# First attention: the value products of four key blocks placed one at a time between the score steps

## What is computed

```python
Q, K, V = (proj(W_Q), proj(W_K), proj(W_V))          # 16 heads of 16 features
Q = _apply_rope(Q, cos, sin); K = _apply_rope(K, cos, sin)
scores = jnp.einsum('bhsd,bhtd->bhst', Q, K) / jnp.sqrt(jnp.float32(D_K))
scores = jnp.where(causal[None, None], scores, -jnp.inf)
attn = jax.nn.softmax(scores, axis=-1)
out = jnp.einsum('bhst,bhtd->bhsd', attn, V)
```

## Time and profile before

| | us |
|---|---|
| median of 3 runs | 1461.62 |
| lowest, highest | 1457.1, 1462.15 |
| profiled execution | 1458.09 |
| its span | 1456.4 |

### The profile page before, as it was taken

How to read it: one execution, slowest core, us unless ns; L and a number is a source line. 1 busy time by engine, 2 the same in 40 slices (tenths; PEclk the granted TensorE clock), 3 DMA queues, 4 the chain that set the end, 5 groups by cost and what they waited for, 6 DMA issues and landing times. The chain is left out here.

```text
span 1456.4 us, 29479 instructions
## 1 busy us (share of the span) xinstructions
PE 1237.8 (85%) x9695; PEld 969.9 (67%) x9696; DVE 850.5 (58%) x1794; ACT 660.5 (45%) x1260; POOL 666.6 (46%) x616
## 2 busy tenths in 40 slices
PE   5886999999978959944998786798869999999996
PEld 3664555555547747732766666788847888878885
DVE  4897788888738849985554684433323333333332
ACT  2881666666755534420445552233213433333332
POOL 6865777776351304876000000454224554444553
PEclk9996899999999968775999998999979999999998
DMA  2487999999300025654442420000174334554331
GB/s 54 141 277 248 259 285 270 274 275 286 69 1 1 1 82 162 195 159 91 111 110 51 144 73 8 18 26 30 37 285 133 57 60 127 134 133 131 56 50 20
DMA packets 122865, 179.26 MB, mean 123 GB/s; under 512 B 26052, under 2 KB 83820, under 8 KB 122772
## 3 DMA queue, kind: packets, MB, share of 16 engines
q1 hardware_dynamic: 105876, 159.62, 37.6%
q0 software_dynamic: 16896, 18.44, 7.5%
HBM read 104.73 MB, written 74.31 MB: 123 GB/s over the span
## 5 line engine op out<-in xcount | busy, mean ns | idle before, releaser
L1635 DVE TENSOR_REDUCE att_top<-att_psS 128x4 f32<-128x512 f32 (+2 forms) x192 | 195.0, 1037 | 45.2 <-PE att_psS L1522 42.2
L2786 POOL DMA_INDIRECT out<-ffn1c_y,ffn1c_table x72 | 113.4, 1575 | 180.4 <-ACT ffn1c_y L2899 112.3
L2927 DVE TENSOR_TENSOR ffn1c_hid<-ffn1c_psG,ffn1c_sil 128x512 f32<-128x512 f32 x72 | 49.8, 692 | 145.6 <-PE ffn1c_psG L2827 145.6
L1606 ACT ACTIVATE att_prob<-att_psS 128x1024 f32<-128x1024 f32 (+1 forms) x96 | 83.3, 887 | 63.0 <-PE att_psS L1536 63.0
L1516 PE MATMUL att_psS<-pairs_ka,pairs_qa 48*128 48x384 f32 (+3 forms) x512 | 100.0, 399 | 11.8 <-DMA pairs_ka<-k_parts 7.2
L2827 PE MATMUL ffn1c_psG<-ffn1c_w_h,ffn1c_xh 128*128 x288 | 98.0, 422 | 11.1 <-DMA ffn1c_w_l<-experts_lo 6.0
L2435 POOL DMA_INDIRECT slots<-ffn1b_entry,ffn1b_sloti x64 | 62.9, 983 | 92.1 <-ACT ffn1b_act_h L2648 52.6
L1606 ACT ACTIVATE pairs_part<-att_psS 128x1024 f32<-128x1024 f32 (+1 forms) x96 | 83.0, 889 | 35.8 <-PE att_psS L1536 35.8
L2775 POOL DMA_INDIRECT ffn1c_rows<-normed_rows,ffn1c_table x72 | 71.2, 988 | 46.6 <-DVE ffn1c_gate L2947 22.9
L2827 PE MATMUL ffn1c_psG<-ffn1c_w_l,ffn1c_xh 128*128 x288 | 91.4, 399 | 0.0
L2827 PE MATMUL ffn1c_psG<-ffn1c_w_h,ffn1c_xl 128*128 x288 | 91.1, 398 | 0.0
(11 more groups left out here) (397 smaller groups left out, 3518.4 us busy)
## 6 DMA issues: line engine op xcount, KB each, us to landing
prep_raw<-in_w_all SPq DMA_DIRECT2D x27, 512.0 KB, 5.6
experts_hi<-ffn0w_room SPq DMA_DIRECT2D x27, 512.0 KB, 5.9
experts_lo<-prep_lo SPq DMA_DIRECT2D x27, 512.0 KB, 7.4
ffn1c_w_h<-experts_hi SPq DMA_DIRECT2D x8, 1536.0 KB
ffn1c_w_l<-experts_lo SPq DMA_DIRECT2D x8, 1536.0 KB
qkv_near<-near_keys SPq DMA_DIRECT2D x32, 320.0 KB, 4.3
q_parts<-pairs_part SPq DMA_DIRECT2D x8, 1024.0 KB
k_parts<-pairs_part SPq DMA_DIRECT2D x16, 512.0 KB
```

Of the source, the lines that this page charges most:

```text
L1606: act.activation(dst, src, ACT.Exp, scale=0.25).then_inc(s["exp"], 1)
L1635: dve.tensor_reduce(dst, src, AX.X, ALU.max).then_inc(s["max"], 1)
L2786: pool.indirect_dma_start(out=rows_out, in_=y[:, t.buf, :], in_offset=None, out_offset=bass.IndirectOffsetOnAxis(ap=table[:, t.value:t.val ...
L2927: dve.tensor_tensor(hid[:, t.par, :], psG[:, t.par, 1, :], sil[:, t.par, :], ALU.mult).then_inc(s["act"], 1)
```

## The change

In TensorE's loop, the value products of blocks 1 and 2 get places of their own. Before, blocks 0 and 1 stand together behind query step 5, and blocks 2 and 3 together behind query step 2 of the next round. After, block 0 stands behind query step 5, and blocks 1, 2 and 3 behind query steps 0, 1 and 2 of the next round; each is followed by the key step of the same n. Nothing else changes.

```diff
                     if n == 5 and 0 <= u - 3 < NU:
                         values(u - 3, 0)
-                        values(u - 3, 1)
-                    if n == 2 and 0 <= u - 4 < NU:
-                        values(u - 4, 2)
-                        values(u - 4, 3)
+                    if n < TG - 1 and 0 <= u - 4 < NU:
+                        values(u - 4, n + 1)
                     if 0 <= u - 3 < NU:
                         key_scores(u - 3, n)
```

## The result

The changed kernel takes 1466.84 us in the median of 11 runs (1459.38 to 1477.65), the kernel before 1461.62 in as many (1456.9 to 1464.01). The ratio is **1.0046**, 95% interval 1.0028 to 1.0063: 5.2 us slower by the medians and 6.7 by the ratio, with 4.1 to 9.2 us as its interval: outside the noise of so many runs, and too near to half a per cent to say on which side it lies. The forecast was 1466. The profiled execution took 1467.21 us, its span is 1465.5.

What follows compares the result with a forecast made beforehand. TensorE's own occupancy was taken as the bound. +0.38 us a unit gave +10.3 over 27 periods; with -2.5, -2.0 and +0.4 that is +6.2 us, put at 1466 us between two starting points, range 1456 to 1476.

Steps and rivals of the forecast that it cites:

- The bound: Attention stage: TensorE's own occupancy, about 8.05 us of each 8.49 us unit, sets the pace; two places wait.
- the period: Sign of being right: copies at L1612 some 8.8 to 8.9 us apart, where they are 8.49.
- 0.175 us in a group: Fixed cost of each group of value products, whatever it holds; four groups instead of two add 0.35 us a unit.
- 0.12 at the entry: Extra time from marks into a value group rather than a score step; two more entries add 0.24 us a unit.
- Exits: Rival: leaving a value group also costs 0.10, two more a unit, 1471 to 1473 us; chance 0.10.
- The two waits: TensorE's waits at query step 1 and key step 3 shrink, giving back 0.10 and 0.11 us a unit.
- The offsets: Savings over the stage against the longer units: irregular units -2.5 us, the drain at its end -2.0 us.
- the half-clock start: First value products run at half clock, where two more groups cost again: +0.4 us.
- Free groups: Rival: added groups cost nothing, a unit is at best 8.28 us, total 1456 to 1457 us; chance 0.22.
- The late clock: Rival: block 0 alone fails to bring full clock, up to 7.6 us per unit, about 1474 or 1489; chance 0.12.
- POOL: Block 2, wanted 1.14 us sooner, might wait for POOL's clip: taken as 0, between 0 and 0.3 us.

Runs made afterwards that it cites:

- half_marks: Changed kernel with one of the two halves of the causal marks left out, 16 matmuls fewer a unit: 1445.87 us, kernel before 1442.4.
- rows_late_before: Kernel before, with VectorE's two instructions on the turned maxima moved from behind its step 1 to behind step 2: 1468.93 us, kernel before 1465.59.
- one_group: Kernel before, with all four value blocks in one group behind query step 2 of the next round: 1514.29 us, kernel before 1465.59.
- both halves: Kernel before with only block 1 moved behind query step 0, or only block 2 behind query step 1: 1468.5 and 1467.92 us, kernel before 1465.59.
- turn_between: rows_late_before with the turning of the maxima put between value blocks 2 and 3: 1440.44 us, kernel before 1442.4.
- block1_moved: Kernel before with only block 1 moved, behind query step 0, blocks 2 and 3 still together: 1468.5 us, kernel before 1465.59.
- rows_late_after: Changed kernel with VectorE's two instructions on the turned maxima behind its step 2: 1462.06 us, kernel before 1437.44.

## Why the prediction was right

- **The bound.** TensorE's occupancy plus one wait for VectorE: shown by half_marks and rows_late_before. one_group adds what the sum did not need: this holds only while no group is longer than the ring can cover. Of the signs set down beforehand, the period did not come: 8.715 us, where 8.8 to 8.9 was to show it right.
- **0.175 us in a group:** the four groups of a unit take 2.82 against 2.50, +0.32 for a forecast of +0.35. **0.12 at the entry:** 0.22 and 0.22 at the new places, +0.22 against 0.24. **Exits:** nothing, key step 2 after a group still 0.28; that rival falls.
- **The two waits** are the terms that were mis-sized. Query step 1 gave back 0.17 and not 0.10: I had taken the whole of its 0.65 us as its own, but its first part had waited too (0.23 where 0.13 is enough). Key step 3 gave back 0.17 and not 0.11; the maximum of step 2 begins 0.34 behind its marks (378.49 to 378.83), and I had 0.40, read at step 0. So a unit is +0.225 and not +0.38, and 27 of them 6.1 us and not 10.3.
- **The offsets** were over-counted as well, which is why the total held: irregular units gave back 0.7 and not 2.5, the drain 0.9 and not 2.0. In the drain ScalarE's period hardly moved (6.34 against 6.38): one block less stands before step 5, but the same block then stands before step 0. Only the end, 5.04 against 5.97, kept its 0.9. The total of the stage, 4.5, and the median's 5.2 against a forecast of 6.2 and a centre of 4.4 above the median, is a sum in which two errors of 4.2 and 2.9 us stood against each other (and 0.4 for the half-clock start, which the first copy at 158.84 doesn't show).
- **Free groups** fell by both halves and turn_between. **The late clock** did not happen in the changed kernel's profile, and it is no dead rival. Of the four profiled kernels that have block 0 alone behind query step 5, three reach the full clock 1.6 to 2.1 us after the first value product (the changed kernel, block1_moved, half_marks), and rows_late_after after 21 us. In the ten others, with two or four blocks there, it takes 1.8 to 4.5 us. One case in four doesn't show that the lone block is the cause, but the price was real, some 8 us, more than the whole difference measured here; only one of the eleven runs of the changed kernel has a profile, so that it rose early in that one is in part luck.
- **POOL** played no part: from 158 to 397 us of the changed kernel no value product waits for it, where the weight loads of the kernel before waited 5.4 us in 14 places.

## What to carry to other kernels

Where matmuls with different tilings of the array take turns, count the visits and not only the columns: here each visit of the value products cost about 0.3 us whatever it held, before what the waits gave back, and a finer interleaving, which fills the idle time of engines that are not the bound, is paid by the one that is. Price such an edit by start-to-start distances of groups with different sizes, and check it on a third. A wait that an order shows belongs to that order: recompute it for the new one before you credit or charge it.

## What the runs showed of the hardware that I had not expected

- When the full clock comes varies more than the order of the work suggests. With TensorE busy for 4.93 of 5 us in 145 to 150 us of the changed kernel, score steps had left it at half; it rose 1.8 us after the first value product there, 3.3 after it in the kernel before, and 21 after it in rows_late_after, in which TensorE was busy for 5.00 of 5 us in each window from 150 to 170 us.
- The same unit with the same waits can keep the full clock or lose it: in one_group TensorE was busy for 2.31 of 3 us (163 to 166 us) and stayed at full clock, and for 2.36 and 2.49 of 3 (372 to 378 us) and fell to half in the next window. The kernel before and the changed one never fall in this stage once they are up.
- Taking work or waits off TensorE did not shorten the stage while the DMA engines were busy. From the first copy to the 28th the kernel before takes 232.46 us at 8.49 a clean unit and rows_late_before 239.56 at 8.16; the changed kernel takes 237.81 at 8.715 and half_marks 238.11 at 8.38. The cause isn't shown: these are single profiles on three chips, and in rows_late_before the clock fell twice.
